# First stage of a two-layer kernel: x in three loads, value weights loaded by themselves, value products between turns and router products

## The chip, the cores and the metric

The kernel runs on one core of a Trainium2 chip. The metric is the device time of one execution in microseconds (us); the profile's times count from the start of the span, which is the time from the first to the last instruction of the profiled execution.

The engines are named as the profile names them: PE is the matrix engine (PEld its weight loads, which overlap its products), DVE the vector engine, ACT the scalar engine, POOL the general engine, and SP issues most of the transfers. Each engine takes its own instructions from a list of its own, written out by hand in the program, and waits on semaphores that the others raise.

## What is computed

Two layers of the same form: the rows are normalised, one branch is attention, the other a gated mixture of experts, and their product is added to x. The change is in the beginning of the first layer:

```python
x = L0_attn_x                      # 4 x 256 rows of 256
xn = _layernorm(x, axis=-1)
s = _L0_attn_ref(xn, L0_attn_Wq, L0_attn_Wk, L0_attn_Wv, L0_attn_Wo)
g = _silu(_L0_ffn_ref(xn, L0_ffn_router_weight, L0_ffn_router_bias, ...))
x = x + s * g
# within _L0_attn_ref
q = apply_rope(proj(Wq)); k = apply_rope(proj(Wk)); v = proj(Wv)
# within _L0_ffn_ref: 16 experts, four to a row
logits = x @ router_weight.T + router_bias
top_val, top_idx = jax.lax.top_k(logits, TOP_K)
gate_up = jnp.einsum('th,ehd->etd', x, gate_up_proj) + gate_up_proj_bias[:, None, :]
```

The kernel does not compute all 16 experts for every row. It sorts the rows by expert into 40 tiles of 128 rows and runs each tile with its own expert's weights, so the first stage also has to make lists: which row goes into which tile, and which expert owns a tile.

## The kernel before

The 1024 rows are eight row tiles of 128. **Loads.** SP issues, in this order (lines 444 to 461): x rows 0 to 3 (in row tiles), the identity matrix, x rows 4 to 7, the router's weights, the other constants, the router's bias, the query, key and value weights in one load of 768 KB, then biases, the rotation tables and the down weights.

**Rows.** DVE takes the moments of row tiles 0 to 3 (`variances`, lines 1572 to 1581), ACT takes the square root (line 721), DVE the reciprocal and the normalised rows (`rows_normal`, lines 1586 and 1588), and then the same for 4 to 7. Before x is there, PE runs 18 products of ones with ones (`dense`, line 1384) that nobody reads.

**PE's list in the first stage** is `route` (line 1091). A turn (line 1003) transposes a row tile through PE and ACT copies it back (line 695). A router product (line 1014) gives 16 logits for each row. After the turns and router products of all eight row tiles come the value products, `narrow` (line 1025: one row tile times the 256 value columns, four records of the trace each), which ACT copies out (line 701), and between them the counts (`count`, lines 1059 to 1064), which sum over the rows how many chose each expert. A count p needs DVE's choice of row tiles 2p and 2p+1. Then come the query and key products, `wide` (line 1041: eight of them, each two halves, four records of the trace in all), and between those `place` (line 1086), which makes the list of rows by tile, and `tile_experts` (line 1079), which makes the list of owners.

**DVE's list** after the rows is the choice of four experts for each pair of row tiles (lines 1601 to 1622), then, once the last count is done, a chain of small operations from line 1650 on that ends in four pairs of one-hot matrices (lines 1698 and 1700), which `place` multiplies. The list of rows is written at line 1693 (`gidx`), the owners at line 1710.

**After the lists** POOL gathers the rows of the tiles (line 588), and SP fetches the weights of the tiles' owners (line 484, 512 KB each). PE's first tile turn (line 1235) stands behind seven of the eight wide products, and its first expert product (line 1258) behind all eight. The 40 tiles follow in a loop, then attention, then the second layer.

What sets the order is the hand-written lists alone; there is no planner. ACT's list has the copies of the turns, then those of the eight value products, then copies of one-hot matrices (line 740) and of the wide products (line 706).

Of the kernel before, what the change touches and what calls it, by code (L numbers as in the profile page):

```python
# [15 lines left out]
P = 128  # L16
D = 256
# [86 lines left out]
def build_program(nc, x, consts, wqkv0, wo0, wr0, rb0, gub0, dnb0, gu0, dn0,  # L104
# [4 lines left out]
    with ctx:  # L109
# [3 lines left out]
        def sem(name):  # L113
            return ctx.enter_context(nc.semaphore(name))
# [169 lines left out]
        s_x = [sem(f"x_in{h}") for h in range(2)]  # L284
# [149 lines left out]
        VALUES_AT = 33  # L434
        EARLY_ROWS = ((0, 4), (4, 6), (6, 8))
# [6 lines left out]
        def _(sp):  # L442
            x_rows = x.rearrange("(t p) d -> p t d", p=P)
            sp.dma_start(xr[:, 0:4, :], x_rows[:, 0:4, :]).then_inc(s_x[0], 16)
            sp.dma_start(cst[:, 0:P], consts[:, 0:P]).then_inc(s_id, 16)
            sp.dma_start(xr[:, 4:8, :], x_rows[:, 4:8, :]).then_inc(s_x[1], 16)
            sp.dma_start(wqkv_sb[:, :, 3 * D:3 * D + E0], wr0).then_inc(s_wr, 16)
            sp.dma_start(cst[:, P:], consts[:, P:C_END]).then_inc(s_cst, 16)
            sp.dma_start(rb0_sb[:, :], rb0.partition_broadcast(P)).then_inc(s_rb, 16)
            sp.dma_start(wqkv_sb[:, :, 0:3 * D], wqkv0).then_inc(s_wqkv, 16)  # L450
# [234 lines left out]
        def _(ac):  # L685
# [29 lines left out]
            def turn_and_project(s):  # L715

                if s.n == 0:
                    for i in range(NTT):
                        if i % 4 == 0:
                            ac.wait_ge(s.ve_ready, i // 4 + 1)  # L720
                            ac.activation(sd[:, i:i + 4], sd[:, i:i + 4], ACT.Sqrt).then_inc(s.sd_ready, 1)
                        turned(s, i)
                        ac.dma_start(xn_dram[0][i * P:(i + 1) * P, :], xn[:, i, :]).then_inc(s.xn_stored, 16)
                    for i in range(NTT):
                        narrow(s, i)
                    columns = ((0, 1, 2, 3), (4, 5, 6, 7))
                else:
                    for i in range(4):
                        narrow(s, i)
                    for i in (6, 7):  # L730
                        turned(s, i)
                    for i in range(4, NTT):
                        narrow(s, i)
                    wide(s, 0)
                    columns = ((0,), (1, 2, 3, 4, 5, 6, 7), ())
# [256 lines left out]
        def _(pe):  # L992
# [13 lines left out]
            def router(s, i):  # L1006

                pe.wait_ge(s.xnT_ready, i + 1)
                if i == 0:
                    pe.wait_ge((s_wr, s_wqvu1)[s.n], (16, 32)[s.n])  # L1010
# [8 lines left out]
            def narrow(s, i):  # L1019

                if i == 0 and s.n == 0:
                    pe.wait_ge(s_wqkv, 16)
# [68 lines left out]
            def route(s):  # L1091

                if s.n == 0:
                    pe.wait_ge(s_id, 16)
                    for i in range(NTT + 1):
                        if i == 4:
                            dense(5, 5)
                        if i < NTT:
                            turn(s, i)
                        if i >= 1:  # L1100
                            router(s, i - 1)
                    narrow(s, 0)
                    narrow(s, 1)
                    count(s, 0)
                    count(s, 1)
                    narrow(s, 2)
                    count(s, 2)
                    count(s, 3)
                    for i in range(3, NTT):
                        narrow(s, i)  # L1110
# [14 lines left out]
                wide(s, 0)  # L1125
                if s.n == 0:
                    for i in (0, 1, 2):
                        place(s, i)
                    wide(s, 1)
                    for i in (3, 4, 5):  # L1130
                        place(s, i)
                    wide(s, 2, (0,))
# [3 lines left out]
                    wide(s, 2, (1,))  # L1136
                    wide(s, 3)
                else:
                    wide(s, 1)
# [247 lines left out]
            dense(18, 2)  # L1387
# [166 lines left out]
        def _(ve):  # L1554
# [17 lines left out]
            def variances(s, h):  # L1572

                ve.wait_ge(s_x[h], 16)
                for i in range(4 * h, 4 * h + 4):
                    ins = ve.bn_stats(bnst[:, i, :], xr[:, i, :])
# [595 lines left out]
```

## Time and profile before

| | us |
|---|---|
| median of 3 runs | 414.98 |
| these runs | 413.81, 414.98, 415.04 |
| the profiled execution | 413.56 |
| its span | 411.8 |

In the profile, a busy share is an average over the whole span. The first stage lasts from 0 to about 39 us, a tenth of it, so it has to be read by itself: by the chain that ended last, by the engines' instructions in order of time, and by the granted clock of short stretches. The rows of those views are in the section on rows below.

### The profile page before, as it was taken

How to read it: one execution, taken by the hardware profiler on the slowest of the kernel's cores; microseconds unless marked ns; L12 is line 12 of the kernel's file. 1: busy time of each engine (PE TensorE's matmuls, PEld its weight loads, DVE VectorE, ACT ScalarE, POOL GpSimd, SP SyncE). 2: the span in 40 equal slices, each digit the busy share in tenths (PEclk: the TensorE clock that was granted, in tenths of full speed). 3: DMA queues.
4: the chain of work that ended last, by engine and by line, in shares of the span. 5: the costliest groups of instructions: out<-in, count | busy, mean ns of one | idle time of the engine just before them, and what ended most of it. 6: DMA issues, size and time to landing. Idle time of an engine off the chain costs nothing.

```text
span 411.8 us, 9630 instructions
## 1 busy us (share of the span) xinstructions
PE 395.2 (96%) x3059; PEld 291.1 (71%) x3059; DVE 315.9 (77%) x1070; ACT 231.7 (56%) x583; POOL 211.5 (51%) x205
## 2 busy tenths in 40 slices
PE   8999999999999999799998899999999999999995
PEld 4765797797787787466666678468778776566684
DVE  5886788887988556679999988766788972545895
ACT  3273244344344446789999953645777767524731
POOL 2104487776774210588785410177777720677710
PEclk9899999999999999889999999999999999999999
DMA  7948888889899998279688874034666644333322
GB/s 232 392 179 274 289 267 293 287 283 315 286 331 296 296 310 273 72 174 206 159 196 217 224 281 164 1 92 125 180 188 184 186 133 139 88 98 108 90 69 73
DMA packets 41073, 82.84 MB, mean 201 GB/s; under 512 B 6928, under 2 KB 26000, under 8 KB 40384
## 3 DMA queue, kind: packets, MB, share of 16 engines
q1 hardware_dynamic: 29792, 60.59, 44.2%
q0 software_dynamic: 9600, 19.93, 19.5%
q10 hardware_dynamic: 1632, 1.71, 1.3%
q8 instruction: 26, 0.43, 0.4%
q14 instruction: 23, 0.19, 0.1%
HBM read 65.42 MB, written 14.68 MB: 195 GB/s over the span
## 4 chain that ended last, share of the span: by engine, by line
PE 87%; DVE 9%; issue 2%; DMA 1%; ACT 1%; ACTq 0%; DVEq 0%
PE ps L1258 14%; PE ps L1197 8%; PE ps L1478 7%; PE ps L1297 6%; PE ps L1401 5%; PE ps L1224 5%; PE ps L1376 4%; PE ps L1025 3%; PE ps L1041 3%; PE ps L1489 3%; PE ps L1253 3%; PE ps L1183 3%; PE ps L1044 2%; PE ps L1235 2%; PE ps L1289 2%
## 5 line engine op out<-in xcount | busy, mean ns | idle before, releaser
L588 POOL DMA_INDIRECT til<-xn_rows,gidx x64 | 64.0, 1000 | 84.5 <-PE ps L1235 36.8
L911 ACT ACTIVATE til<-til,mxs 128x128 f32<-128x128 f32 (+1 forms) x128 | 49.0, 452 | 0.0
L1258 PEld LDWEIGHTS ps<-til,experts 128*128 128x128 f32 x384 | 45.3, 192 | 4.8 <-DVE til L1823 2.4
L1258 PE MATMUL ps<-til,experts 128*128 128x128 f32 x384 | 47.8, 278 | 0.7 <-issue 0.3
L763 ACT ACTIVATE til<-ps 128x256 f32<-128x256 f32 x40 | 15.3, 383 | 57.2 <-PE ps L1235 57.1
L1947 DVE CUSTOM_DVE_ANT_0 til<-ps,cst 128x128 f32<-128x128 f32 (+1 forms) x128 | 37.9, 353 | 6.5 <-PE ps L1376 5.8
L812 ACT ACTIVATE til<-ps,wtile 128x256 f32<-128x256 f32 x88 | 38.8, 469 | 4.3 <-PE ps L1226 2.4
L1199 PE MATMUL ps<-xn,til 128*64 128x192 f32 x192 | 33.8, 329 | 0.0
L1197 PE MATMUL ps<-experts,til 128*64 x192 | 33.7, 329 | 0.0
L1401 PE MATMUL ps<-cst,til 128*128 128x128 f32 x192 | 28.9, 289 | 4.5 <-DVE til L1956 3.6
L1297 PE MATMUL ps<-experts,til 128*128 x128 | 33.1, 381 | 0.0
L1401 PEld LDWEIGHTS ps<-cst,til 128*128 128x128 f32 x192 | 21.4, 146 | 13.9 <-issue 9.3
L647 POOL DMA_INDIRECT experts<-sorted_rows,slotu x16 | 25.3, 1582 | 8.8 <-DMA experts<-sorted_rows,slotu 4.8
L1197 PEld LDWEIGHTS ps<-experts,til 128*64 128x64 f32 x192 | 25.3, 137 | 5.0 <-issue 2.6
L1478 PE MATMUL ps<-att,experts 128*128 128x512 f32 x64 | 28.6, 594 | 0.0
L634 POOL DMA_INDIRECT rou<-sorted_rows,slotu x16 | 15.2, 952 | 23.3 <-DMA sorted_rows<-til 18.7
L1199 PEld LDWEIGHTS ps<-xn,til 128*64 128x64 f32 x192 | 25.3, 137 | 0.0
L647 POOL DMA_INDIRECT rou<-sorted_rows,slotu x16 | 20.4, 1278 | 8.1 <-issue 4.0
L1297 PEld LDWEIGHTS ps<-experts,til 128*128 128x128 f32 x128 | 21.8, 190 | 2.0 <-issue 0.3
L1224 PE MATMUL ps<-experts,til 96*64 x96 | 22.7, 379 | 0.5 <-ACT til L812 0.5
L1820 DVE TENSOR_SCALAR til<-ps,bcol 128x128 f32<-128x128 f32 x32 | 11.1, 347 | 15.7 <-PE ps L1258 15.4
L1825 DVE SCALAR_TENSOR_TENSOR til<-til 128x256 f32<-128x256 f32 x32 | 20.9, 653 | 1.1
(278 smaller groups left out, 1038.5 us busy)
## 6 DMA issues: line engine op xcount, KB each, us to landing
experts<-in_gu SPq DMA_DIRECT2D x32, 512.0 KB, 5.2
sorted_rows<-til SPq DMA_DIRECT2D x88, 128.0 KB, 2.2
att<-in_gu SPq DMA_DIRECT2D x16, 512.0 KB, 6.1
experts<-in_gu SPq DMA_DIRECT2D x8, 768.0 KB, 5.3
experts<-in_dn SPq DMA_DIRECT2D x4, 1024.0 KB, 11.6
experts<-in_dn SPq DMA_DIRECT2D x8, 384.0 KB, 6.4
experts<-att SPq DMA_DIRECT2D x44, 32.0 KB
xr<-in_x SPq DMA_DIRECT2D x2, 512.0 KB, 4.3
```

What stands on the lines that cost most here:

```text
L588: po.indirect_dma_start(to, None, xn_dram[s.n], bass.IndirectOffsetOnAxis(ap=gidx[:, at:at + 1], axis=0))\
L647: po.indirect_dma_start(rows[:, i, :], None, ys_dram[s.n], bass.IndirectOffsetOnAxis(ap=slotu[s.n][:, i * TOPK + k:i * TOPK + k + 1], axis=0),
L812: ac.activation(ybuf[:, j, :], y, ACT.Copy, scale=wtile[:, at:at + 1])\
L911: ins = ac.activation(pr[h % len(pr)][:, cols], pr[h % len(pr)][:, cols], ACT.Exp, bias=mxs[:, h % len(pr), tt:tt + 1], scale=-1.0)
L1197: pe.matmul(ps[0:HALF_ROWS, 2 + p % 2, at], xgT1[:, p % 2, c, k, 0:HALF_ROWS], gu[:, bass.ds(e * (KD * w) + k * w, w)], start=(k == 0), st ...
L1199: mm = pe.matmul(ps[HALF_ROWS:P, 2 + p % 2, at], xgT1[:, p % 2, c, k, HALF_ROWS:P], gu_second[t % 4][:, k * w:(k + 1) * w], start=(k == 0) ...
L1224: pe.matmul(ps[0:HALF_ROWS, 6 + p % 2, at], hT1[:, p % 2, c, 0:HALF_ROWS], dn[0:F1, bass.ds(e * D, D)], start=True, stop=True)
L1258: mm = pe.matmul(ps[:, b0, m * P:(m + 1) * P], gw[n][:, k * w + m * P:k * w + (m + 1) * P], xgT[:, j % 2, k, :], start=(k == 0), stop=(k = ...
L1297: mm = pe.matmul(ps[:, 6 + j % 2, 0:D], hT[0:s.FP, j % 2, k, :], dn[0:s.FP, bass.ds(e * (s.KF * D) + k * D, D)], start=(k == 0), stop=(k = ...
L1401: mm = pe.transpose(ps[:, 4 + h % 2, n * P:(n + 1) * P], pr[h % len(pr)][:, n * P:(n + 1) * P], ident)
L1478: mm = pe.matmul(ps[:, n % 2 + 2 * w, :], wsgu_sb[:, k, w * SH + m * P:w * SH + (m + 1) * P], L[1].xnT[:, k, h * 512:(h + 1) * 512], start ...
L1947: ve.tensor_tensor_reduce(out=pr[h % len(pr)][:, cols], in0=ps[:, h % 4, cols], in1=maskz[:, (1 - tt) * P:2 * P], scale=1.0, scalar=3.0e38 ...
```

## The change

SP loads x in three parts: row tiles 0 and 1, 2 and 3, 4 to 7; the identity stands behind the second part. The value columns of the weights are loaded by themselves (256 KB) right behind the router's weights and raise the same semaphore; the first router product waits for both. The query and key columns (512 KB) come where the whole was. `variances` waits for the first two parts one after the other.

PE runs 15 products of ones ahead of the first turn, not 18, and the five in the middle of the turns are gone. The value product of row tile i-3 stands behind the turn of row tile i and the router product of row tile i-1. After the loop come the value product of row tile 6, counts 0 and 1, the value product of row tile 7, count 2, the first half of the first wide product, and count 3. From there on each wide product stands one place earlier: the first two are ahead of the first `place`, the third ahead of the fourth, and half of the fourth ahead of the seventh.

ACT copies a value product out behind each turn from the fourth on.

```diff
         VALUES_AT = 33
+        NARROW_LAG = 3
+        X_PARTS = ((0, 2), (2, 4), (4, 8))
...
-            sp.dma_start(xr[:, 0:4, :], x_rows[:, 0:4, :]).then_inc(s_x[0], 16)
-            sp.dma_start(cst[:, 0:P], consts[:, 0:P]).then_inc(s_id, 16)
-            sp.dma_start(xr[:, 4:8, :], x_rows[:, 4:8, :]).then_inc(s_x[1], 16)
+            for part, (t0, t1) in enumerate(X_PARTS):
+                sp.dma_start(xr[:, t0:t1, :], x_rows[:, t0:t1, :]).then_inc(s_x[part], 16)
+                if part == 1:
+                    sp.dma_start(cst[:, 0:P], consts[:, 0:P]).then_inc(s_id, 16)
             sp.dma_start(wqkv_sb[:, :, 3 * D:3 * D + E0], wr0).then_inc(s_wr, 16)
+            sp.dma_start(wqkv_sb[:, :, 2 * D:3 * D], wqkv0[:, :, 2 * D:3 * D]).then_inc(s_wr, 16)
             sp.dma_start(cst[:, P:], consts[:, P:C_END]).then_inc(s_cst, 16)
             sp.dma_start(rb0_sb[:, :], rb0.partition_broadcast(P)).then_inc(s_rb, 16)
-            sp.dma_start(wqkv_sb[:, :, 0:3 * D], wqkv0).then_inc(s_wqkv, 16)
+            sp.dma_start(wqkv_sb[:, :, 0:2 * D], wqkv0[:, :, 0:2 * D]).then_inc(s_wqkv, 16)
...
                         turned(s, i)
                         ac.dma_start(xn_dram[0][i * P:(i + 1) * P, :], xn[:, i, :]).then_inc(s.xn_stored, 16)
-                    for i in range(NTT):
+                        if i >= NARROW_LAG:
+                            narrow(s, i - NARROW_LAG)
+                    for i in range(NTT - NARROW_LAG, NTT):
                         narrow(s, i)
...
                 if i == 0:
-                    pe.wait_ge((s_wr, s_wqvu1)[s.n], (16, 32)[s.n])
+                    pe.wait_ge((s_wr, s_wqvu1)[s.n], 32)
...
-                if i == 0 and s.n == 0:
-                    pe.wait_ge(s_wqkv, 16)
...
                     for i in range(NTT + 1):
-                        if i == 4:
-                            dense(5, 5)
                         if i < NTT:
                             turn(s, i)
                         if i >= 1:
                             router(s, i - 1)
-                    narrow(s, 0)
-                    narrow(s, 1)
+                        if i >= NARROW_LAG:
+                            narrow(s, i - NARROW_LAG)
+                    narrow(s, 6)
                     count(s, 0)
                     count(s, 1)
-                    narrow(s, 2)
+                    narrow(s, 7)
                     count(s, 2)
+                    wide(s, 0, (0,))
                     count(s, 3)
-                    for i in range(3, NTT):
-                        narrow(s, i)
...
-            dense(18, 2)
+            dense(15, 2)
...
-                ve.wait_ge(s_x[h], 16)
-                for i in range(4 * h, 4 * h + 4):
-                    ins = ve.bn_stats(bnst[:, i, :], xr[:, i, :])
+                for part, (t0, t1) in enumerate(X_PARTS):
+                    if t0 // 4 == h:
+                        ve.wait_ge(s_x[part], 16)
+                        for i in range(t0, t1):
+                            ins = ve.bn_stats(bnst[:, i, :], xr[:, i, :])
```

How the lists read at the three places that matter. The line numbers of the changed program are a few higher: 1009 is the turn, 1020 the router product, 1029 the value product, 1045 the wide product, 1065 the count, 1090 `place`. First PE from the last turn to the first count, before:

```order
L1003 MATMUL ps<-cst,xn 128x128 x2
L1014 MATMUL ps<-wqkv,att 128x16 x4
L1025 MATMUL ps<-wqkv,att 128x256 x4
L1059 MATMUL ps<-mcnt,tri_bf 128x16
L1061 MATMUL ps<-mcnt,ones_bf 128x128
```

and in the changed program:

```order
L1009 MATMUL ps<-cst,xn 128x128 x2
L1020 MATMUL ps<-wqkv,att 128x16 x2
L1029 MATMUL ps<-wqkv,att 128x256 x2
L1020 MATMUL ps<-wqkv,att 128x16 x2
L1029 MATMUL ps<-wqkv,att 128x256 x4
L1063 MATMUL ps<-mcnt,tri_bf 128x16
```

The first three rows of the second listing stand five times in a row there, once for each turn from the fourth to the eighth; seven value products stand ahead of the first count, where there were two. Next PE from the third count to the first `place`, before:

```order
L1061 MATMUL ps<-mcnt,ones_bf 128x64
L1061 MATMUL ps<-mcnt,ones_bf 128x48
L1061 MATMUL ps<-mcnt,ones_bf 128x32
L1061 MATMUL ps<-mcnt,ones_bf 128x16
L1064 MATMUL ps<-mcnt,tri_bf 128x112
L1025 MATMUL ps<-wqkv,att 128x256 x10
L1041 MATMUL ps<-att,experts 128x512 x2
L1086 MATMUL ps<-til,rou 128x40 x12
```

and in the changed program:

```order
L1065 MATMUL ps<-mcnt,ones_bf 128x64
L1065 MATMUL ps<-mcnt,ones_bf 128x48
L1045 MATMUL ps<-att,experts 128x512
L1065 MATMUL ps<-mcnt,ones_bf 128x32
L1065 MATMUL ps<-mcnt,ones_bf 128x16
L1068 MATMUL ps<-mcnt,tri_bf 128x112
L1045 MATMUL ps<-att,experts 128x512 x3
L1090 MATMUL ps<-til,rou 128x40 x12
```

Between the last count and the first `place` there were five value products and a wide product; now there are a wide product and a half. Last ACT around the second square root, before:

```order
L695 ACTIVATE att<-ps 128x2x128
L723 DMA xn_rows<-xn 128x256
L721 ACTIVATE sd<-sd 128x4
L695 ACTIVATE att<-ps 128x2x128
L723 DMA xn_rows<-xn 128x256
```

and in the changed program:

```order
L699 ACTIVATE att<-ps 128x2x128
L727 DMA xn_rows<-xn 128x256
L705 ACTIVATE att<-ps 128x256
L725 ACTIVATE sd<-sd 128x4
L699 ACTIVATE att<-ps 128x2x128
```

The copy of the first value product (L705) has come between the copy of the fourth turn and the square root.

## Rows read from the trace of the kernel before

**Rows 1.** The page: busy time by engine, and the last-ended chain by engine.

```profile
PE 395.2 (96%) x3059; PEld 291.1 (71%) x3059; DVE 315.9 (77%) x1070; ACT 231.7 (56%) x583; POOL 211.5 (51%) x205
...
PE 87%; DVE 9%; issue 2%; DMA 1%; ACT 1%; ACTq 0%; DVEq 0%
```

**Rows 2.** The chain that ended last, 0 to 50 us: start, duration, what.

```profile
0.73 3.64 DMA xr<-in_x
...
4.40 1.42 DVE bnst L1576 x4
...
8.34 0.62 PE ps L1014 x4
...
10.32 1.09 PE ps L1384 x5
11.41 0.22 PE ps L1003 x2
...
12.72 0.26 PE ps L1003 x2
12.98 0.35 PE ps L1014 x4
...
14.69 3.42 PE ps L1025 x8
...
19.52 4.38 PE ps L1025 x20
...
26.10 1.81 PE ps L1041 x4
...
29.66 7.73 PE ps L1041 x18
37.39 0.22 PE ps L1235 x2
...
39.33 1.78 PE ps L1258 x16
```

**Rows 3.** PE by stretches: length, busy (instructions), granted clock, DMA share, GB/s.

```profile
14.00:14.50 0.50, 0.50 (x5) 1.00 1.02 426
...
15.00:15.50 0.50, 0.50 (x3) 0.50 1.07 440
...
17.50:18.00 0.50, 0.50 (x4) 0.50 1.00 414
```

**Rows 4.** DVE in order of time: start, duration, engine, line, operation.

```profile
19.56 0.17 DVE L1650 TENSOR_SCALAR nts<-ps 128x16 f32<-128x16 f32 x1 [0.27 <-PE ps L1064]
...
24.25 0.69 DVE L1700 TENSOR_TENSOR rou<-iota_mid,slot_mid 128x1024 f16<-128x1024 f16 x1
...
25.09 0.69 DVE L1700 TENSOR_TENSOR rou<-iota_mid,slot_mid 128x1024 f16<-128x1024 f16 x1
...
29.68 0.20 DVE L1693 SCALAR_TENSOR_TENSOR gidx<-ps,wtile 128x40 uint32<-128x40 f32 x1
```

**Rows 5.** ACT in order of time.

```profile
10.26 0.21 ACT L721 ACTIVATE sd<-sd 128x4 f32<-128x4 f32 x1
...
23.93 0.38 ACT L701 ACTIVATE att<-ps 128x256 f32<-128x256 f32 x1 [0.48 <-PE ps L1025]
```

**Rows 6.** SP's issues in order of time.

```profile
1.25 0.48 SPq L445 DMA_DIRECT2D cst<-in_consts  x1
...
2.99 0.59 SPq L448 DMA_DIRECT2D cst<-in_consts  x1
...
31.52 2.10 SPq L484 DMA_DIRECT2D experts<-in_gu  x4
```

**Rows 7.** Transfers issued from 0 to 45 us: count, size, us from issue to landing.

```profile
experts<-in_gu SPq DMA_DIRECT2D x6, 512.0 KB, 5.2
...
cst<-in_consts SPq DMA_DIRECT2D x1, 326.5 KB, 4.9
...
cst<-in_consts SPq DMA_DIRECT2D x1, 64.0 KB, 3.7
```

More of the change, by code:

```diff
@@ L281, in build_program @@
         psf = ps[:, :, :].rearrange("p b n -> p (b n)")
-        s_x = [sem(f"x_in{h}") for h in range(2)]
+        s_x = [sem(f"x_in{h}") for h in range(3)]
         s_cst, s_wr, s_bias, s_wqkv, s_dn0, s_w1, s_wqvu1, s_small1, s_tab1 = map(sem, (
@@ L1124, in route @@
                     narrow(s, 7)
-                wide(s, 0)
                 if s.n == 0:
+                    wide(s, 0, (1,))
+                    wide(s, 1)
                     for i in (0, 1, 2):
                         place(s, i)
-                    wide(s, 1)
+                    wide(s, 2)
                     for i in (3, 4, 5):
                         place(s, i)
-                    wide(s, 2, (0,))
+                    wide(s, 3, (0,))
                     place(s, 6)
@@ L1135, in route @@
                     tile_experts(s)
-                    wide(s, 2, (1,))
-                    wide(s, 3)
+                    wide(s, 3, (1,))
                 else:
+                    wide(s, 0)
                     wide(s, 1)
```

## The prediction

> **What bounds the kernel now.** I read the page first: PE is busy 96% of the span, and 87% of the chain that ended last is PE [rows 1]. The program is one queue of PE work, so an edit counts if it moves the moment at which PE starts the tile loop. That is the first expert product at 39.33 us, with the tile's turn at 37.39 us ahead of it [rows 2]; from there PE's chain goes on almost without a break. I read the chain from 0 to 50 us next. It starts with the load of x (landed at 0.73 + 3.64 = 4.37 us) and DVE's moments (1.42 us), and from the first router product at 8.34 us it is PE's up to the tile loop [rows 2]. But a PE that never idles need not be what sets the pace: in the order of time, DVE waits only 0.27 us for the last count, whose sums it reads at 19.56 us [rows 4], and PE then fills the time in which DVE makes the one-hot matrices with five value products (4.38 us) and a wide one [rows 2]. So two chains run side by side, nearly balanced, and they meet at the last count and at `place`. The third view is the clock: it stands at 0.50 of full, 1.2 instead of 2.4 GHz, in the stretches from 15 to 18 us, after PE had done nothing but turns and router products since 11.41 us [rows 2, 3].
>
> **Prices.** A value product costs 4.38 / 5 = 0.88 us at full clock. A wide product costs 7.73 / 4.5 = 1.72 us, half of one 0.86. A turn and a router product are 0.26 + 0.35 = 0.61 us. The two value products at 1.2 GHz took 3.42 us, so this fall of the clock cost 3.42 - 1.75 = 1.67 us [rows 2]. The three counts' worth of products between 14.69 and 19.52 us is what remains of 4.83 us after 3.42 and one more value product, 0.5 us.
>
> **Loads.** The second part of x now ends the 512 KB that the first load was, and is issued in the place of the identity, at 1.25 us [rows 6]. Bounds: the same bytes had landed at 4.37 us [rows 2], and the identity, issued there, landed at 1.25 + 3.7 = 4.95 us [rows 7]. I take 4.65, between them. DVE has the moments of the first two row tiles by then and needs 1.42 / 2 = 0.71 us more: 5.4 instead of 5.8 us, so 0.4 us gained (0.1 to 0.7).
>
> The Trainium skill, "DMA: Bandwidth & Descriptors", section "Anatomy of one DMA — SWDGE (gpsimd) path", puts a transfer at about 2.0 us plus its bytes at 436 GB/s. By that, as an estimate, 256 KB would land 2.6 us after the issue and the gain here would be 1.0 us instead of 0.4. The trace does not agree: its 64 KB took 3.7 us and its 512 KB 3.64 [rows 2, 7], where the rule has 2.15 and 3.2, so I stay with the rows.
>
> The first router product now also waits for the value columns. It would start at 8.34 - 0.4 = 7.9 us. The 326.5 KB of constants, issued at 2.99 us, landed at 7.89 [rows 6, 7] with 1430 KB up to their end (x 1024, identity 64, router's weights 16, constants 326.5); the value columns end at 1360 KB. I take no wait, with 0.3 us as the upper bound. The three products of ones that go at the start ran while PE waited for x: nothing. The other loads are issued 0.5 to 1.3 us later; the constants and the query and key columns are used after 12 us and around 22 us, which hides that.
>
> **The value product ahead of the square root.** This is the added wait. On ACT the copy of the first value product stands ahead of the square root for row tiles 4 to 7, and behind that root stand DVE's reciprocal and rows, and PE's fifth turn. The product starts where the products of ones did, 10.32 - 0.4 = 9.92 us, ends at 10.80, its copy takes 0.38 us from 0.03 us after that (in the trace the last such copy starts at 23.93 us, the products end at 23.90) [rows 2, 5], and the root comes at 11.23 us instead of 10.26 [rows 5]. The fifth turn follows at 11.41 + 0.97 = 12.38 us. The 0.4 us gained is gone, and PE stands idle from 10.80 to 12.38 us; the 1.09 us of products of ones that went away [rows 2] filled just this hole.
>
> **Up to the last count.** From 12.38 us PE has four turns and five router products (4 x 0.61 + 0.35 = 2.79 us), seven value products (6.13), half a wide product (0.86) and the counts (0.5): 22.66 us. Before it was 19.52 us [rows 2], so the last count is 3.1 us later, although nothing in this sum runs at 1.2 GHz any more. DVE cannot hide it: everything behind the count on its list waits for it. Bounds: 0.5 us less, if weight loads of turns run under value products, 0.4 us more, if the steps keep waits for ACT's copies.
>
> **From the last count to the tile loop.** DVE needs as long as before: the first pair of one-hot matrices ends 24.94 - 19.56 = 5.38 us after its read of the count, the second 0.84 us later [rows 4], so at 28.1 and 28.9 us. PE has only a wide product and a half to do meanwhile, 2.58 us, and stands from 25.2 us on. In the kernel before, five value products and a wide one filled this time. The third `place` ends at 29.05 us, where before it ended at 26.10. From there to the tile's turn it was 37.39 - 26.10 = 11.29 us of PE work; now one wide product less is left, 9.57 us. The turn comes at 38.6 us, **1.2 us later** than before (bounds 0.4 to 2.0). The list of rows (29.68 us before [rows 4]) comes 2.95 us later too. The first weights are issued at 31.52 + 2.95 = 34.5 us and land 5.2 us later [rows 6, 7], at 39.7; the expert product needs them at 40.5, so that cover shrinks from 2.6 to 0.8 us but holds.
>
> **The clock.** The sum has no stretch at 1.2 GHz, while the 413.56 us of the profiled execution hold one in the first stage. In the changed list there are two candidates. From 7 to 12.4 us PE does four turns, three router products and one value product and then stands 1.6 us; from 25.2 to 29.05 us it does three `place` groups and nothing else. The stretch in the trace that had a fall behind it was 3.28 us of turns and router products [rows 2]; the second candidate is longer and emptier. A fall costs at most the 1.67 us measured, and nothing where it lies in a hole; I take 1.3.
>
> **The rivals.**
>
> *One fall of the clock*: 1.2 + 1.3 = 2.5 us slower, 417.5 us. For it: the two lean stretches. This is my forecast, chance 0.40.
>
> *No fall*: 1.2 us slower, 416.2 us. For it: before, the clock still stood at full speed from 14.0 to 14.5 us, after 2.6 us of turns and router products [rows 2, 3]. Chance 0.28.
>
> *A fall in both places*: 1.2 + 2.6 = 3.8 us slower, 418.8 us. Chance 0.21.
>
> *Value products hide among turns and router products*, the other side: if a turn's and a router product's time is mostly weight loads that run under a value product's streaming, a value product costs about half there, 0.44 us. Then the last count comes 7 x 0.44 = 3.1 us earlier than in my sum, at 19.6 us, everything behind it moves with it, and the tile's turn comes at 35.5 us: 1.9 us faster, 413.1 us. It decides in favour of the change from a last count at 20.3 us, that is 0.54 us for a value product. Against it: the five in a row took 0.88 us each with PE never waiting [rows 2], and the hole in front of the fifth turn stays. Chance 0.11.
>
> *The split of x gains nothing* (the second part lands at 4.95 us) belongs to the bounds: 0.3 us on each case.
>
> **How the numbers follow.** The sum moves the profiled execution's 413.56 us (span 411.8 us and 1.76 us around it), which is 1.42 us below the median of the runs shown; I put the difference on the median: 414.98 + 2.5 = 417.5 us. The range leaves out the hiding case (0.11), and the outer ends of no fall and of two falls (0.08 together): 415.0 to 419.2 us. A measurement of this kernel can tell about 0.3%, 1.24 us, from no change. Faster than that is the hiding case, 0.10. Within it: no fall up to its middle and a little beyond, 0.28. Slower: 0.62.
>
> **What would show it.** In the profile after: the square root of row tiles 4 to 7 (line 725 now) behind the first value copy, near 11.2 us; the last count's end near 22.7 us and DVE's read of it (L1655) waiting more than 2 us for PE; PE idle for some 3 us ahead of the first `place`; the tile's turn near 38.6 us at full clock, near 39.9 with one fall; a granted clock of 0.50 in a stretch behind one of the two holes and none at the old place. I am wrong if the last count ends before 20.3 us, or if PE has no hole ahead of `place`, or if the tile loop behind it takes up the delay, for which I see no wait in the chain.

## The result and the profile of the changed kernel

| | before | changed |
|---|---|---|
| median, us | 414.53 | 419.74 |
| runs, us | 412.35 to 415.04 | 416.88 to 422.60 |
| ratio, 95% interval | | 1.0125 [1.0071, 1.0180] |
| the profiled execution, us | 413.56 | 420.53 |
| its span, us | 411.8 | 418.7 |
| first expert product, us | 39.33 | 46.09 |
| the span behind that, us | 372.5 | 372.6 |

The change makes the kernel 1.25% slower, 5.2 us where 2.5 were forecast, and 419.74 lies above the range's end of 419.2. The last two rows place the loss: of the 6.9 us by which the spans differ, 6.76 are there when the tile loop begins; the rest of the program neither adds to them nor takes them up. The profiled executions stand 7.0 us apart, the medians 5.2: the one of the changed kernel is 0.8 us above its median, the one of before 1.0 below its own. Below, ratios are formed from undisturbed runs alone, so that a ratio need not be the quotient of the medians beside it.

The page, busy time by engine, is nearly what it was [rows 1]: PE's work is the same and the span longer.

```profile
PE 395.8 (95%) x3051; PEld 290.4 (69%) x3051; DVE 315.2 (75%) x1070; ACT 231.0 (55%) x583; POOL 211.1 (50%) x205
```

The chain that ended last in the first stage (start, duration, what), to be read beside [rows 2]:

```profile
3.46 4.96 DMA wqkv<-in_wqkv
8.42 0.14 issue
8.55 0.59 PE ps L1020 x4
...
10.50 0.97 PE ps L1029 x4
11.47 0.02 issue
11.49 0.38 ACT att L705
11.88 0.10 ACT sd L725
...
12.73 0.44 PE ps L1009 x2
13.17 0.35 PE ps L1020 x4
13.52 0.96 PE ps L1029 x4
...
23.43 0.08 PE ps L1068
...
29.15 0.61 DVE rou L1705
29.76 0.05 issue
29.81 0.31 PE ps L1090 x4
30.12 3.59 PE ps L1045 x4
33.71 0.40 PE ps L1090 x12
34.11 1.83 PE ps L1045 x2
...
37.56 5.23 DMA til<-xn_rows,gidx
42.79 0.14 issue
42.92 0.41 PE ps L1238 x2
43.33 0.80 issue
44.13 1.96 PE ps L1045 x4
46.09 1.78 PE ps L1261 x16
```

It names five places in order: the value columns, for which the first router product (L1020) waits; the value copy (L705) ahead of the square root (L725); the last count (L1068) at 23.51 us; the stretch from 30.12 us, where a wide product (L1045) takes 3.59 us and half of one 1.83, against 1.81 for a whole one before [rows 2]; and, new at the end, the gather of the first rows, which ends last, with 0.80 us behind the tile's turn (L1238) in which PE waited for nothing that the profile shows. Ahead of the third `place` (L1090, 29.81 us) DVE's second pair of one-hot matrices (L1705) ends at 29.76.

DVE (start, duration, then in brackets the idle time ahead and what ended it): where it waited 0.27 us for the last count [rows 4], it now waits 2.30.

```profile
23.53 0.17 DVE L1655 TENSOR_SCALAR nts<-ps 128x16 f32<-128x16 f32 x1 [2.30 <-PE ps L1068]
```

PE in order of time: the hole ahead of the first `place` (2.84 us) and the wait for the gather (0.46).

```profile
28.97 0.56 PE L1090 MATMUL ps<-til,rou 128*128 128x40 f16 x8 [2.84 <-DVE rou L1705]
...
42.92 0.41 PE L1238 MATMUL ps<-cst,til 128*128 128x128 f32 x2 [0.46 <-DMA til<-xn_rows,gidx]
```

PE by stretches (length, busy time and instructions, granted clock, DMA share, GB/s): the clock falls in the hole and stays at 0.50 until about 35.8 us; the old fall at 15 us [rows 3] is gone.

```profile
13.00:23.50 10.50, 10.50 (x69) 1.00 1.02 410
23.50:29.00 5.50, 2.66 (x7) 0.99 0.39 151
29.00:35.50 6.50, 6.22 (x30) 0.50 0.00 0
```

The transfers of the first stage (size, us from issue to landing; [rows 7]): the two parts of x landed in 2.9 us, the value columns in 5.0.

```profile
xr<-in_x SPq DMA_DIRECT2D x2, 256.0 KB, 2.9
...
wqkv<-in_wqkv SPq DMA_DIRECT2D x1, 256.0 KB, 5.0
```

### The profile page after: what moved, and what is told of

Read it like the earlier page. It is cut to its first block, busy times and chain, and to the rows that moved or that the text cites. A ratio compares the mean times of both kernels' runs of the same rounds, so it can differ in the third digit from the quotient of the medians.

```text
span 418.7 us, 9617 instructions
## 1 busy us (share of the span) xinstructions
PE 395.8 (95%) x3051; PEld 290.4 (69%) x3051; DVE 315.2 (75%) x1070; ACT 231.0 (55%) x583; POOL 211.1 (50%) x205
## 4 chain that ended last, share of the span: by engine, by line
PE 82%; DVE 10%; issue 3%; DMA 2%; ACT 1%; SPq 1%; ACTq 0%; DVEq 0%
PE ps L1261 13%; PE ps L1200 7%; PE ps L1481 7%; PE ps L1300 5%; PE ps L1404 5%; PE ps L1227 5%; PE ps L1379 4%; PE ps L1492 3%; PE ps L1029 3%; PE ps L1256 3%; PE ps L1186 3%; PE ps L1048 2%; PE ps L1238 2%; PE ps L1045 2%; PE ps L1292 2%
```

## The experiments

Two theories stood after this profile. **The order**: seven value products ahead of the last count cost time by themselves, since they leave PE too little for the time in which DVE makes the one-hot matrices. **The accidents**: the order is free, and the loss is the wait for the value columns, the copy ahead of the square root, and the clock. "First expert product" is the mark for the first stage throughout: 39.33 us before, 46.09 in the changed kernel. In time, none of the versions with one or two mends (last hole filled, both holes filled, root first, own semaphore, wide product first) nor the one with five value products back is clear of the changed kernel: their intervals overlap its 1.0071 to 1.0180. What they show is read from one trace each.

**The loads alone**: the program of before with the loads of the change and 15 products of ones.

> The kernel before with the changed loads alone (x in three parts, value columns by themselves behind the router's weights and waited for by the first router product, 15 products of ones at the start); the lists of PE and ACT are those of the kernel before, with the five products of ones in the middle. If the loads are harmless: the first turn at 6.7 us instead of 7.46, but the first router product at 8.55 us, held by the value columns, instead of 8.34, so all that follows is 0.0 to 0.3 us later than before and the time is that of before within 0.3 us. Rival, the loads carry part of the loss: more than 1 us slower.

413.68 us, ratio 0.9993 [0.9972, 1.0013]: no difference. The first router product waits here too, and starts at 8.63 us (8.34 before). The chain from 10.75 to 18.94 us is DVE's, first the rows and then the choices of experts, so the last count comes at 19.26 us and the first expert product at 39.08:

```profile
10.75 0.19 DVE rstd L1590
...
18.76 0.19 DVE mcnt L1626
...
19.26 4.38 PE ps L1027 x20
```

There is no fall of the clock in this first stage, and yet it gains only 0.25 us on before, whose two value products at 1.2 GHz had cost 1.67 us. So that fall had cost next to nothing: DVE's choices end at 19 us whether PE is slow or not. The loads by themselves cost nothing here; the loss of the change comes with the order of the lists, and with what the order makes of the waits.

**The last hole filled**: 15 products of ones ahead of the first `place`, to keep PE at work there.

```diff
                     wide(s, 1)
+                    dense(15, 1)
                     for i in (0, 1, 2):
```

> The changed kernel with 15 products of ones (512 columns, nobody reads them) in the hole of 2.8 us ahead of the first place. Nothing else moves. Theory A, the hole lets the clock fall and the fall from 29 to 35.6 us is the largest single loss: no stretch at 0.50 behind 29 us, the wide products between the place groups take 1.7 and 0.9 us again, the first expert product comes 2.5 to 3.3 us earlier than 46.1 us, and the time is about 417 us. Theory B, the order alone (value products ahead of the last count) is the loss and the clock only goes with it: the first expert product stays later than 45 us and the time at 419 to 420 us. Both expect the last count unchanged near 23.5 us.

422.74 us, from 417.33 to 424.47, ratio 1.0127 [1.0074, 1.0180]. The last part did as expected, the wide product between the places took 1.81 us again; but the clock now fell behind the first hole, at 13.7 us, for 10 us, over four steps of turn, router product and value product:

```profile
8.00:13.50 5.50, 3.01 (x21) 1.00 0.96 308
13.50:24.00 10.50, 10.50 (x38) 0.51 1.01 405
```

The last count slid to 29.16 us and the first expert product to 48.94. That the records would keep the clock up was wrong as it was put: with them it did not fall at the one place, and it fell at the other.

**Both holes filled**: beside that, six products of ones behind the first value product.

```diff
                             narrow(s, i - NARROW_LAG)
+                        if i == NARROW_LAG:
+                            dense(6, 5)
```

> The changed kernel with products of ones in both holes: 6 behind the first value product, ahead of the fifth turn, and 15 ahead of the first place. The one-hole version had the clock at 0.50 from 13.6 to 23.9 us, right behind the first hole. Theory A, the holes let the clock fall: now no stretch at 0.50 before 40 us, the first expert product at 43.0 us (the order's own cost stays) and the time at 416 to 417 us, with the runs closer together than the 416.9 to 422.6 us of the changed kernel. Rival, it is the lean turns and router products, not the holes: the clock still falls somewhere between 9 and 24 us and the runs spread as before.

417.89 us, ratio 1.0107 [1.0069, 1.0146]. In part as the rival had it, and not as the theory: the clock still fell behind the first turns and was at 0.57 on average from 10.5 to 14.5 us, so that the six products themselves took 2.56 us and the last count came at 24.88. From there to the tile loop there is no fall; the first expert product is at 44.35.

**The square root first**: ACT's root for row tiles 4 to 7 ahead of the first value copy.

```diff
+                        if i == 4:
+                            narrow(s, 0)
                         turned(s, i)
...
-                        if i >= NARROW_LAG:
+                        if i > NARROW_LAG:
                             narrow(s, i - NARROW_LAG)
```

> The changed kernel with ACT's second square root ahead of the copy of the first value product. If the root's place behind that copy holds DVE's rows back, the root comes at about 10.0 us instead of 11.78, the fifth turn at about 11.5 instead of 12.73 us (PE is busy with the first value product until 11.5) and the last count about 1.2 us earlier, at 22.3 us; the time falls by about 1.2 us against the changed kernel, to 418 to 418.5. Rival: the load of x and of the value columns holds this stretch, the fifth turn does not move and the time stays.

418.33 us, ratio 1.0098 [1.0066, 1.0130]. The fifth turn came at 11.03 us (12.73 in the changed kernel), the last count at 21.75 (23.51), the first expert product at 42.64. Of these 3.45 us, 1.76 are there at the last count. Not all of them are the root's: in this execution the value columns landed 4.3 us after their issue and not 5.0, and the first router product started at 8.10 us and not 8.55; without these 0.45 us the root's place is worth 1.31, near the 1.2 expected. Most of the rest is the clock, which fell in the hole again, but for 3.4 us only: the wide product took 3.07 us, and the half one behind it 0.95, where the changed kernel's took 3.59 and 1.83.

**An own semaphore for the value columns**: the first router product no longer waits for them, the first value product does.

```diff
-            sp.dma_start(wqkv_sb[:, :, 2 * D:3 * D], wqkv0[:, :, 2 * D:3 * D]).then_inc(s_wr, 16)
+            sp.dma_start(wqkv_sb[:, :, 2 * D:3 * D], wqkv0[:, :, 2 * D:3 * D]).then_inc(s_wv, 16)
...
-                    pe.wait_ge((s_wr, s_wqvu1)[s.n], 32)
+                    pe.wait_ge((s_wr, s_wqvu1)[s.n], (16, 32)[s.n])
...
+                if i == 0 and s.n == 0:
+                    pe.wait_ge(s_wv, 16)
```

> The changed kernel with a semaphore of their own for the value columns: the first router product waits for the router's weights alone, the first value product for the value columns. If the wait for the value columns (landed at 8.42 us) costs what it seems to, the first router product comes at about 7.6 us instead of 8.55, the fifth turn at 11.8 instead of 12.73, the last count 0.9 us earlier than 23.5 and the time falls by 0.9 us. Rival: the first value product waits for the same columns anyway or the router's weights land late too, and less than 0.4 us is gained.

418.42 us, ratio 1.0128 [1.0083, 1.0174]. First router product 7.71 us instead of 8.55, last count 22.65 instead of 23.51: the wait was worth 0.86 us, all of which arrives at the count. The time does not show it, the ratio is that of the changed kernel. The clock fell in the hole for about 3.4 us (the wide product 3.22), and the first expert product is at 44.05. One of the accidents is thus priced, and it is a small part of the loss.

**The last wide product ahead of the tile's turn.** In before, PE has no gap around the tile's turn; here the gather and the 0.80 us stand open. The wide product that PE does behind the turn might cover them; `last_wide` runs ahead of the turn, in the list of a tile's steps.

```diff
-                def begin(t, j):
+                def last_wide(t, j):
                     if t == 0:
                         wide(s, NTT - 1)
+
+                def begin(t, j):
+                    if t == 0 and s.n == 1:
+                        wide(s, NTT - 1)
```

> The changed kernel with the eighth wide product ahead of the first tile's turn and not behind it. Theory C, the loss at the end of the stage is cover: the gather of the first rows lands 5.2 us after its issue and PE has too little work left behind the lists, then PE's queue runs dry and the register reads behind the turn show with 0.8 us. Then with 1.72 us more work ahead of the turn the wait of 0.46 us and the gap of 0.8 us go, the first expert product comes about 1 us earlier than 46.1 us and the time is about 418.6. Rival: another wait takes their place (ACT's copy of the turned rows, about 0.6 us, now stands uncovered between turn and first expert product), and nothing or less than 0.5 us is gained.

420.08 us, ratio 1.0167 [1.0132, 1.0202]. In the trace both gaps are gone; ACT's copy of the turn shows instead:

```profile
34.51 7.89 PE L1045 MATMUL ps<-att,experts 128*128 128x512 f32 x18
42.24 0.38 PE L1238 MATMUL ps<-cst,til 128*128 128x128 f32 x2
43.09 2.05 PE L1261 MATMUL ps<-til,experts 128*128 128x128 f32 x16 [0.47 <-ACT til L769]
```

From the end of the owners' product to the first expert product it is 8.42 us (from 34.67), in the changed kernel 9.64 (from 36.45): 1.2 us recovered, of which the expert product gives back 0.27 (2.05 us and not 1.78). The time of the kernel shows nothing of it. The span was 416.8 us, 1.9 less than the changed kernel's, and the runs spread over 5 us, more than the effect; so the gain is shown in the trace and not in the median.

**Five value products back behind the counts**: only the first three stay among the turns, the rest is as in before.

```diff
-                        if i >= NARROW_LAG:
+                        if NARROW_LAG <= i < NARROW_LAG + 3:
                             narrow(s, i - NARROW_LAG)
...
+                    for p in range(4):
+                        count(s, p)
+                    for i in range(3, NTT):
+                        narrow(s, i)
```

> The changed kernel with only the value products of row tiles 0 to 2 between the turns; the other five, the counts and the wide products stand as in the kernel before (five value products and a whole wide product behind the last count, counts in a row). Loads and ACT's first copies are those of the changed kernel. Theory B, value products ahead of the last count make the lists late: the last count comes at 20.5 to 21 us, held by DVE's choices and no more by PE, no hole ahead of place, no fall of the clock behind it, the first expert product at 40 to 40.5 us and the time at 414.5 to 415.5. Rival, the loads and the square root behind the copy carry most of the loss: the first expert product not before 42 us, the time above 417.

417.60 us, ratio 1.0118 [1.0075, 1.0160]. As expected the last count came at 20.3 us, held by DVE's choices, and there was no hole ahead of `place`. But PE now stood before the counts, and the clock fell behind that: the five value products took 6.07 us, not 4.38.

```profile
16.50:20.50 4.00, 1.95 (x20) 1.00 1.02 413
20.50:24.50 4.00, 4.00 (x13) 0.57 1.04 426
```

The first expert product is at 41.62 us, 39.9 without the fall: 0.6 us over before. The time is what the rival expected, above 417, and the first expert product lies between the two; only with the fall taken off does it fit the theory. So the order decides when the last count comes, and here the clock fell again behind a stretch in which PE had stood.

**Three mends at once**: own semaphore, root first, and the 15 products of ones ahead of `place` (the text below calls them one product; they are 15). The edits are those above; what is left of the change is its order.

> The changed kernel with three mends at once: the value columns raise a semaphore of their own, so that the first router product no longer waits for them (worth about 0.9 us when done alone); ACT's square root for row tiles 4 to 7 ahead of the first value copy (worth about 1.8 us at the last count when done alone); and one product of ones, 16 records, in the hole ahead of the first place. What is left is the order of the list: seven value products ahead of the first count. Theory (the order costs time by itself, apart from its holes and from the clock): fifth turn near 10.3 us, last count near 21 us (before 19.5), no fall of the clock in the first 40 us, tile's turn near 39 us with its wait for the gather and the register reads behind it uncovered, first expert product near 41.5 us against 39.33 before; 415.5 to 416.5 us. Rival (the loss is the two waits and the clock, and the order is free): last count near 19.5, first expert product at 39.5 or sooner, 413.5 to 414.5 us. If the clock falls all the same at the first turns, the records ahead of the last count show it, and the first expert product is to be read less what they took too long.

415.94 us, ratio 1.0042 [1.0023, 1.0061]. No fall of the clock in the first stage: the granted clock is 1.00 in all four stretches of it,

```profile
8.00:16.00 8.00, 7.73 (x52) 1.00 0.97 323
16.00:24.00 8.00, 8.00 (x44) 1.00 1.02 412
24.00:32.00 8.00, 7.76 (x58) 1.00 0.23 92
32.00:40.00 8.00, 6.76 (x18) 1.00 0.63 211
```

and still the last count is at 21.98 us and the first expert product at 41.72, 2.4 us later than before. The end of the stage shows half of it, and the start a part:

```profile
1.21 6.33 PE ps L1393 x15
7.53 0.23 PE ps L1012 x2
...
33.21 5.21 DMA til<-xn_rows,gidx
38.42 0.14 issue
38.55 0.41 PE ps L1244 x2
38.96 0.80 issue
```

The gather holds the turn for 0.44 us and the 0.80 us stand behind it, 1.24 together; the tile's turn itself is 1.16 us late. This speaks for the order: without the hole, the wait for the columns and the fall the kernel stays slower than before, clear of the interval. But the run holds one delay that is not the order's. The fifth turn came at 11.21 us and not at 10.3: the copy of the fourth turn (9.76 to 10.13 us) stood ahead of the root on ACT, and DVE waited 0.99 us for the root. That copy was late because the first turn was: the 15 products of ones at the start (L1393) took 6.33 us here and held PE until 7.53, where the changed kernel's took 5.28 and its first turn came at 6.70. The next version has the same list up to the fifth turn; there they took 5.06 us, and the fifth turn came at 10.58, 0.63 us earlier. The expectation had also added the root at 1.8 us, 0.45 too much (see above).

**The value products shared out**: own semaphore, root first; one value product behind the third router product and one behind the sixth, four among the counts, two behind the last count, with two wide products behind those. The half wide product between the places stands behind them, so the last five `place` follow one another and the list of rows comes sooner.

```diff
+                        if i in (3, 6):
+                            narrow(s, i // 3 - 1)
+                    narrow(s, 2)
+                    narrow(s, 3)
                     count(s, 0)
                     count(s, 1)
+                    narrow(s, 4)
                     count(s, 2)
+                    narrow(s, 5)
                     count(s, 3)
+                    narrow(s, 6)
+                    narrow(s, 7)
...
+                    wide(s, 0)
                     wide(s, 1)
...
-                    for i in (3, 4, 5):
+                    for i in (3, 4, 5, 6, 7):
                         place(s, i)
-                    wide(s, 3, (0,))
-                    place(s, 6)
-                    place(s, 7)
                     tile_experts(s)
-                    wide(s, 3, (1,))
+                    wide(s, 3)
```

> A version made from what the runs showed: the changed loads with a semaphore of their own for the value columns, ACT's second square root ahead of the first value copy, the value product of row tile 0 behind the third router product and that of row tile 1 behind the sixth, four more among the counts, the last two and two wide products behind the last count, the third wide product ahead of the fourth place, the remaining places in a row. Expected: the fifth turn at 10.6 us, the last count at 18.5 us with DVE's choices and PE's products ending together, no hole ahead of place, the list of rows at 27.7 us, the first tile's turn near 34.5 us and the first expert product near 36.5 us instead of 39.3 before: 411.5 to 412.5 us, faster than before. If it fails, the clock falls in the turns (first expert product 38 us or later), or the gather's landing 6 us behind the list and the register reads hold the tile's turn (35 us and a gap of 0.8 us).

412.82 us, ratio 0.9978 [0.9952, 1.0003]. Last count 19.14 us, third `place` 25.71, no fall of the clock in the first stage, first expert product 37.66: 1.7 us ahead of before. The median gains less, and the interval still touches one. **With the sixth value product moved behind the last count as well:**

```diff
-                    narrow(s, 5)
                     count(s, 3)
+                    narrow(s, 5)
```

> The version with the value products shared out, with the sixth value product behind the last count and no longer ahead of it. There PE still stood about a microsecond ahead of the first place, and DVE waited 0.38 us for the last count. Theory (PE's list has just enough behind the count to fill DVE's time): last count 0.3 us earlier, near 18.8 us, no hole ahead of the first place, first expert product near 37.2 us (37.66 without the move, 39.33 before), 411.5 to 412.5 us, clear of the kernel before by 0.4% or more. Rival (the time won in the first stage is given back at the clock's fall between the tile loop and attention, which was longer in the version before this): first expert product as said, but 413 to 414 us, no different from the kernel before.

412.38 us, ratio 0.9952 [0.9930, 0.9973]: faster than before, and the lowest median of all. The way there was not the one expected. The hole ahead of `place` is gone, but the last count came at 19.30 us, no earlier, because DVE's choices end at 18.98 and hold it:

```profile
18.80 0.19 DVE mcnt L1632
18.98 0.05 issue
19.03 0.21 PE ps L1070 x2
19.24 0.07 PE ps L1073
19.30 2.65 PE ps L1034 x12
21.96 3.43 PE ps L1050 x8
```

and the first expert product is at 38.06 us, 0.4 later than in the version before it. There DVE's choices had ended 0.3 us sooner; here the first router product came at 7.93 us, there at 7.54, though nothing had changed ahead of it. The two intervals overlap, so that the last move did something is not shown. Both profiled executions give back part of their gain later: between 160 and 200 us, at the passage from the tile loop to attention, their mean granted clock was 0.87, in the kernel before 0.91, 4% of 40 us or 1.6 us. But this stretch holds a fall in every trace, and its mean clock varies: 0.83 with root first, 0.96 with the own semaphore, 0.91 in the changed kernel. So it blurs every difference of whole times here, and that the new order makes the fall longer is not shown.

## Why the prediction failed in size

**The sign and the mechanism up to `place` were right; three terms of the sum were not.** The later last count, DVE's wait for it, the hole and a fall of the clock behind it came as forecast. What failed is the price of the fall (1.3 us forecast, 2.76 measured), the wait for the value columns (put at 0, worth 0.86 at the last count), and the end of the stage, where the sum followed PE and the weights and left out the gather (0.46 us of wait and 1.23 behind it). Step by step, as the prediction put them:

| step | forecast, us | measured, us |
|---|---|---|
| gain from the split of x | 0.4 (0.1 to 0.7) | 0.8 |
| first router product waits for value columns | 0 (up to 0.3) | starts 8.55, not 7.9 |
| square root of row tiles 4 to 7 | 11.23 | 11.78 |
| fifth turn | 12.38 | 12.73 |
| last count ends | 22.66 | 23.51 |
| DVE waits for it | over 2 | 2.30 |
| PE's hole ahead of `place` | some 3 | 2.84 |
| third `place` ends | 29.05 | 30.12 |
| price of a fall of the clock | 1.3 | 2.76 |
| tile's turn, with one fall | 39.9 | 42.92 |
| first expert product | 41.8 | 46.09 |

The last forecast is 39.33 plus the 2.5 of the sum. Its error of 4.3 us in the profiled execution is 1.07 up to the third `place`, 1.46 at the clock, 0.46 at the gather and 1.23 behind the turn (0.80 and the longer turn and wide product, 0.19 and 0.24), with 0.04 left over.

**The value columns.** The step that took no wait, with 0.3 us as the bound, failed: it reasoned from bytes in the queue and from one neighbour, the constants. The columns landed at 8.42 us, 0.5 us after what the constants had done in before, and what was gained at x made the router product ready earlier. The run with a semaphore of their own puts the wait at 0.86 us at the last count, and the last count missed its forecast by 0.85. That without the wait the sum comes out so well there (22.65 us measured, 22.66 forecast) is luck: the fifth turn came 0.51 us sooner than forecast (11.87), and the way from there took 0.50 longer, since the seven value products cost 6.60 us and not 6.13. The other 0.2 of the 1.07 us at `place` is a slip in the sum: it let the third `place` end some 0.15 us behind DVE's second pair (28.9 and 29.05), where the rows of before have 0.32 (25.78 and 26.10 [rows 2, 4]) and 0.36 was measured (29.76 and 30.12). Nor does the wait come in every execution: with root first, wide product first and five back, which have the same semaphore, the columns landed 4.3 to 4.5 us after their issue, and the first router product did not wait for them.

**The end of the stage.** The sum looked at the weights' cover (2.6 us, down to 0.8) and took the rest as moving with PE. It did not follow the list of rows any further. The trace of before had the row; POOL's gather, in order of time:

```profile
30.77 1.17 POOL L588 DMA_INDIRECT til<-xn_rows,gidx  x1 [18.16 <-DVE selc L1712]
```

With the 5.23 us to the landing that the changed kernel shows, this gather would have landed at 36.0 us, 1.4 us ahead of the turn at 37.39 [rows 2]. The list came 2.95 us later in the sum, the turn only 1.2: the cover was gone by 0.35 us in the sum's own numbers, and 0.46 was measured. It costs more than itself, since the 0.80 us appear behind the turn in the traces in which PE waited there for the gather (the changed kernel, last hole filled, both holes filled, root first, own semaphore, three mends: 0.79 or 0.80 each, behind waits of 0.16 to 0.65) and not where it did not wait (before, loads alone, five back). With wide product first, 0.47 us stand open there, up to ACT's copy; the two shared-out versions, which did not wait either, have 0.27 and 0.49. PE's list has two register reads at that place (L1168 and L1169), which a PE that runs behind its list seems to cover; that they are the 0.80 us was argued and not tried by itself.

**The clock.** The forecast had the right place, one fall in the second hole, and 0.40 for it. Its price was taken from the fall in before, 1.67 us at most. Two things were wrong there. That fall had cost next to nothing to begin with, since DVE's choices end near 19 us with it and without it (the run with the loads alone); so the 413.56 us held no loss that could be set against the new one. And a fall has no fixed length: the traces show 3.4 us (before, square root first, own semaphore, wide product first, both holes filled, five back), 6.8 (the changed kernel) and 10 (last hole filled). At 3.4 us it cost 3.07 - 1.81 = 1.26 and 3.22 - 1.81 = 1.41 us, which is the forecast's 1.3; at 6.8 us it cost (3.59 - 1.81) + (1.83 - 0.95) + (0.40 - 0.30) = 2.76. The six runs of the changed kernel lie between 416.88 and 422.60 us with mean clocks from 0.991 to 0.975, so the median probably holds runs of several lengths; two of the six, at 416.88 and 416.94, even lie under the forecast's 417.5. Only one of them was traced.

**The order itself.** With the mends the first expert product is 2.39 us late. Of these, 1.67 stand at the gather and behind it (0.44 of wait, 0.80, and 0.43 by which the turn and the wide product took longer, 0.41 and 1.96 us for 0.22 and 1.72); without the wait the turn would be 0.72 us late, and 0.63 of that is the start with its products of ones. So, by this estimate, the order by itself costs 2.39 - 0.63 = 1.76 us, nearly all through the late list of rows. The forecast's 1.2 us cannot be held against that: it was for the turn, and with the copy ahead of the root. As an estimate, the prices add up to 0.86 (columns) + 1.31 (root) + 2.76 (clock) + 1.76 (order) = 6.69 of the 6.76 us; they come from different executions, so that so close a fit is partly chance. By this count the order alone is about a quarter, and the accidents that came with it are the rest.

**The split of x** gained 0.8 us, above its bound of 0.7: the moments of row tiles 0 to 3 ended at 3.60 + 1.43 = 5.03 us, before at 5.82 [rows 2], and did not wait for the second part. That the shorter start of 15 products of ones costs nothing held in this trace, where PE waited 0.21 us for the rows; in five others (last hole filled, root first, wide product first, five back, three mends) the 15 took 6.04 to 6.33 us and held the first turn. The two parts landed 2.9 us after their issue. Here the Trainium skill, "DMA: Bandwidth & Descriptors", section "Anatomy of one DMA — SWDGE (gpsimd) path", with its 2.6 us for 256 KB, was nearer than the 3.4 us (4.65 - 1.25) that the sum took from the rows, though that section is on transfers that gpsimd issues and these are SP's. For the value columns, which stood behind other loads, the same size took 5.0.

**The rivals.** Two falls did not occur in one trace; a first stage without a fall occurred only with the three mends together or with another order. That value products hide among turns and router products fell: one took 0.96 us there, more than the 0.88 in a row.

## What to carry over

When two engines run side by side, place work by where the other engine's time ends: before the last count DVE's choices gave PE until about 19 us, behind it DVE's chain needed some 6 us of PE work to cover, and the version nearest to that was the only one clearly faster than the kernel before. When a sum moves a late point, follow every consumer of what is made there, here the gather beside the weights, and compare each cover with the shift of both its ends. A slow stretch in the old trace is a gain for the taking only if the chain that ended last goes through it.

## What the runs showed of the chip

The clock fell behind stretches in which PE had stood part of the time: the page of stretches shows PE busy 2.66 of 5.50 us ahead of the fall in the changed kernel, 3.01 of 5.50 with the last hole filled, 1.95 of 4.00 with five value products back. With the three mends it was busy 7.73 of the 8 us from 8 to 16 us and had no fall. But this is no rule that the runs settle: in before the clock fell after 14.5 us, behind 3.10 us of full work and 4.61 of the 5.40 us ahead of that, and with the loads alone, where PE was busy 3.66 of those 5.40 us, it did not. Where a fall came, and whether it lasted 3.4, 6.8 or 10 us, could be read afterwards but not foretold from the lists. Filling the last hole moved the fall to the first turns twice, and not the third time, with the mends.

The time from issue to landing followed what stood ahead in the queue more than the size: 256 KB took 2.9 us at the head and 5.0 behind other loads, 64 KB 4.0 right behind x. It also varied from one execution to the next: the value columns landed 4.3 to 5.3 us after their issue in the eleven traces with the new loads.

The 15 products of ones at the start, the same in all these traces, took from 4.79 us (both holes filled) to 6.33 (three mends), while the row of the granted clock stands at 1.00 in every one; why is open.
